# Last layer's four experts: twelve dense batch-expert tiles replaced by nine tiles of tokens grouped by expert through DRAM

## The reference, cut to what matters

```
xn = _modulate(_ln(x), sh_mlp, sc_mlp)
gate_logits = xf @ w_gate                                  # 4 experts
topk_logits, topk_idx = jax.lax.top_k(gate_logits, TOP_K)  # TOP_K = 2
gates = jax.nn.softmax(topk_logits, axis=-1)
cw = jnp.sum(jax.nn.one_hot(topk_idx, NUM_EXPERTS, dtype=xf.dtype) * gates[..., None], axis=1)
hmid = jax.nn.gelu(jnp.einsum('tc,ech->eth', xf, w1) + b1[:, None, :], approximate=True)
eo = jnp.einsum('eth,ehc->etc', hmid, w2) + b2[:, None, :]
moe = jnp.einsum('te,etc->tc', cw, eo).reshape(B, N, C)
return x + g_mlp[:, None, :] * moe
```

## Time and profile before

| | |
|---|---|
| median of 3 runs | 1899.22 us (1898.35 to 1902.36) |
| profiled execution, its own time | 1896.54 us |
| its span, first to last instruction | 1894.1 us |
| mean granted TensorE clock | 0.95 |
| last layer's feed-forward windows | 1372.5 us to the end |

### The profile page before, as it was taken

How to read it: one execution, slowest core, us unless ns; L and a number is a source line. 1 busy time by engine, 2 the same in 40 slices (tenths; PEclk the granted TensorE clock), 3 DMA queues, 4 the chain that set the end, 5 groups by cost and what they waited for, 6 DMA issues and landing times.

```text
span 1894.1 us, 27931 instructions
## 1 busy us (share of the span) xinstructions
PE 1738.4 (92%) x9838; PEld 1141.3 (60%) x9838; DVE 1159.2 (61%) x2573; ACT 914.4 (48%) x1635; POOL 577.1 (30%) x567
## 2 busy tenths in 40 slices
PE   6775899998998889998899999999999999999998
PEld 2443444433796634443378764444388899999997
DVE  7863677773555667677436567777445645455454
ACT  2323476667354468675745247676733322222221
POOL 4432122214555323332435232222523301101000
PEclk9997699999999889899899999998999899999999
DMA  7202333331001222323100223333110000100000
GB/s 245 79 2 71 95 105 91 91 112 48 11 1 51 91 82 72 90 70 114 57 11 1 88 67 109 92 100 114 39 38 19 20 25 20 44 10 29 1 26 25
DMA packets 65866, 116.49 MB, mean 61 GB/s; under 512 B 9443, under 2 KB 25235, under 8 KB 65439
## 3 DMA queue, kind: packets, MB, share of 16 engines
q1 hardware_dynamic: 65728, 114.71, 19.6%
HBM read 83.46 MB, written 30.73 MB: 60 GB/s over the span
## 4 chain that ended last, share of the span: by engine, by line
PE 70%; DVE 10%; ACT 7%; issue 4%; DMA 4%; POOL 4%; SPq 2%; DVEq 0%; ACTq 0%; POOLq 0%
PE ps L1696 25%; PE ps L1780 15%; PE ps L1749 8%; PE ps L1735 7%; PE ps L1844 6%; PE ps L1717 5%; ACT Pr L1545 2%; DMA heads_t<-stage 2%; PE ps L1820 1%; DVE negmax L1133 1%; ACT HQ L1520 1%; DVE GT L1059 1%; ACT act L1519 1%; ACT xn L1441 1%; PE ps L1586 1%
## 5 line engine op out<-in xcount | busy, mean ns | idle before, releaser
L1133 DVE TENSOR_REDUCE negmax<-ps 128x1 f32<-128x512 f32 x768 | 488.3, 681 | 221.3 <-PE ps L1717 218.0
L1545 ACT ACTIVATE Pr<-ps 128x512 f32<-128x512 f32 x768 | 410.6, 602 | 208.3 <-PE ps L1735 208.0
L1556 ACT ACTIVATE g<-ps,b1col 128x512 f32<-128x512 f32 x216 | 148.2, 688 | 449.1 <-PE ps L1696 445.0
L1322 DVE CAST G<-g 128x512 fp32r<-128x512 f32 x216 | 122.8, 568 | 280.7 <-ACT g L1556 280.2
L1735 PE MATMUL ps<-QK 55*128 55x512 f32 x768 | 239.5, 515 | 33.4 <-ACT Pr L1545 25.2
L1780 PE MATMUL ps<-W2a,G 128*128 128x288 f32 x1728 | 263.4, 302 | 4.8 <-DVE rowt L1143 4.8
L1780 PEld LDWEIGHTS ps<-W2a,G 128*128 128x128 f32 x1728 | 247.9, 192 | 19.1 <-DVE G L1324 7.3
L1749 PE MATMUL ps<-Pr,V 128*32 128x512 f32 x1536 | 220.0, 646 | 0.0
L1717 PE MATMUL ps<-QK 54*128 54x512 f32 x768 | 196.6, 444 | 18.7 <-DVE negmax L1133 7.0
L1735 PEld LDWEIGHTS ps<-QK 55*128 55x128 f32 x768 | 92.2, 192 | 198.7 <-ACT Pr L1545 103.5
L1324 DVE TENSOR_TENSOR G<-g,G 128x512 fp32r<-128x512 f32 x216 | 170.4, 789 | 7.4
(11 more groups left out here) (221 smaller groups left out, 2241.1 us busy)
## 6 DMA issues: line engine op xcount, KB each, us to landing
QK<-heads_t SPq DMA_DIRECT2D x192, 144.0 KB
heads_t<-stage SPq DMA_DIRECT2D x96, 252.0 KB
QK<-heads_t SPq DMA_DIRECT2D x192, 72.0 KB
raw<-in_w SPq DMA_DIRECT2D x18, 432.0 KB
raw<-in_w SPq DMA_DIRECT2D x12, 576.0 KB
WA<-in_ada_w SPq DMA_DIRECT2D x3, 1728.0 KB
heads_t<-stage SPq DMA_DIRECT2D x24, 144.0 KB
QK<-W1a SPq DMA_DIRECT2D x192, 2.0 KB
```

What stands on the lines that cost most here:

```text
L1133: dve.tensor_reduce(negmax[:, m % 2, h, t:t + 1], ps[:, row_bank(l, s, i), :], AX, ALU.max, negate=True).then_inc(a_free, 1)
L1322: dve.tensor_copy(G[:, n % 3, 0, :], g32[:, n % 2, :]).then_inc(g_hi, 1)
L1545: act.activation(Pr[:, t % 2, 2 * half + pair, :], ps[:, (16 * s + u) % 3, :], ACT.Exp, scale=SCALE).then_inc(b_free, 1)
L1556: act.activation(g32[:, n % 2, :], ps[:, hidden_bank(s), :], ACT.Gelu if l == 1 else ACT.Gelu_apprx_tanh, bias=b1col[:, e, s % FT:s % FT + ...
```

## The change

Batch 0 stays dense (all four experts), and batches 1 to 3 (1536 tokens, 3072 token-expert pairs) are grouped. The feed-forward part of the last layer has 13 windows in place of 16: windows 0, 1 and 2 are batch 0 with experts 0, 1 and 2; windows 3 to 11 are nine tiles of grouped tokens; window 12 is batch 0 with expert 3. Each of the 13 windows has weights of its own, so 13 sets of six pieces are loaded and split in place of 4.

Beside windows 0 to 2, for each batch 1 to 3: `modulate` writes the normed, modulated tokens in token order; the gate is computed turned round (7 matmuls of 512 columns, a copy, four small turns); `rank` counts, by two small matmuls, the place of each token in its experts' regions; `scatter` issues eight indirect DMAs from POOL that write each token's row into the region of each of its two experts in `tok_rows`, and waits for them. `table` then works out which expert and which rows each grouped tile has, and `slots` where each token's two results will be. Each grouped window loads 512 rows (`xg`), transposes them on PE (`lng`), runs as a tile with the weights that the table names, and stores its 512 result rows to `exp_rows`. In window 12, `gather` issues 24 indirect DMAs from POOL that fetch each token's two result rows, and `merge` adds them up on DVE, batch by batch. `tok_rows` (7680 rows of 1408 bytes) is filled with zeros in the prologue by one DMA.

```diff
+LAST, SEL = LAYERS - 1, B - 1
+GROUPED = 2 * SEL + EXPERTS[-1] - 1
...
+WINDOWS = (B, B, GROUPED + EXPERTS[-1])
...
+def raw_slot(n):
+    return n % 2 if n < THREE else (n - THREE) % 3
...
     if v == 0:
+        out += leaving(l) + [(4, "modrow", l, 1, 0), (12, "mod", l, 1, 0)]
+        out += [(14, "gate", l, 0, 0), (15, "gturn", l, 0, 0), (16, "gexp", l, 0, 0), (18, "weigh", l, 0, 0)]
+        out += [(16, "gate", l, 1, 0), (18, "gturn", l, 1, 0), (20, "gexp", l, 1, 0), (21, "rank", l, 1, 0), (23, "weigh", l, 1, 0)]
+        out += [(22, "scatter", l, 1, 0)]
+    if v == 1:
+        out += [(t // 2, "stats2", l, 2, t) for t in range(TT)] + [(2, "mean2", l, 2, 0), (0, "modrow", l, 2, 0)]
+        out += [(8 + c, "ln2", l, 2, c) for c in range(3)] + [(8, "mod", l, 2, 0)]
+        out += [(11, "gate", l, 2, 0), (13, "gturn", l, 2, 0), (15, "gexp", l, 2, 0), (16, "rank", l, 2, 0), (18, "weigh", l, 2, 0)]
+        out += [(17, "scatter", l, 2, 0)]
+        out += [(9 + t // 2, "stats2", l, 3, t) for t in range(TT)] + [(11, "mean2", l, 3, 0), (11, "modrow", l, 3, 0)]
+        out += [(15 + c, "ln2", l, 3, c) for c in range(3)] + [(17, "mod", l, 3, 0)]
+    if v == 2:
+        out += [(0, "gate", l, 3, 0), (2, "gturn", l, 3, 0), (4, "gexp", l, 3, 0), (5, "rank", l, 3, 0), (7, "weigh", l, 3, 0)]
+        out += [(6, "scatter", l, 3, 0), (6, "table", l, 0, 0), (10, "slots", l, 0, 0)]
+    if v + 1 < WINDOWS[l]:
+        first = PIECE["w1", l, v + 1, 0]
+        loads = {0: (-2, -2, 4, 6, 9, 11), 1: (0, 1, 2, 8, 10, 12), 2: (-3, -2, -1, 8, 10, 11)}.get(v, (-3, -2, -1, 8, 10, 12))
+        out += [(t, "load", l, first + q, 0) for q, t in enumerate(loads)]
+        out += [(t, "split", l, first + q, 0) for q, t in enumerate((5, 7, 9, 12, 14, 16) if v > 0 else (1, 3, 7, 9, 12, 15))]
+        out += [(9 if v > 0 else 16, "side", l, v + 1, 0)]
+    if i == -1:
+        out += [(12, "xg", l, 0, 0)] + [(15 + c, "lng", l, 0, c) for c in range(3)]
+    if 0 <= i < GROUPED - 1:
+        out += [(1, "xg", l, i + 1, 0)] + [(11 + 2 * c, "lng", l, i + 1, c) for c in range(3)]
+    if v == WINDOWS[l] - 1:
+        out += [(6, "gather", l, j, 0) for j in range(SEL)]
+        out += [(t, "merge", l, j, part) for j, t in ((0, 16), (1, 20), (2, 21)) for part in range(2)]
         out += [(21, "fin", l, v, 0)]
...
+            sp.dma_start(tok_rows.rearrange("(k p) c -> p k c", p=128),
+                         act32[:, 0, 0:CW].unsqueeze(1).broadcast_to([128, XROWS // 128, CW])).then_inc(zero_out, 16)
...
+            sp.wait_ge(zero_out, 16)
...
+            def tile_load(l, v):
+                sp.wait_ge(xs_out, ALL_XS)
+                if v >= 2:
+                    sp.wait_ge(misc_full, MISC["lng", l, v - 2, 2] + 1)
+                row = 0
+                if v > 0:
+                    sp.wait_ge(table_ready, 1)
+                    row = sp.value_load(tab[0:1, 1, v - 1:v], min_val=0, max_val=XROWS - N)
+                sp.dma_start(XG[v % 2][:, :, :], tok_rows[bass.ds(row, N), :].rearrange("(t p) c -> p t c", p=128)).then_inc(xg_in[v % 2], 16)
+            def tile_store(l, v):
+                sp.wait_ge(acc_free, TT * (WBASE[l] + FRONT + v + 1))
+                sp.dma_start(exp_rows[N * v:N * v + N, :].rearrange("(t p) c -> p t c", p=128), rowt[:, :, :]).then_inc(ys_out, 16)
...
+                elif kind == "scatter":
+                    pool.wait_ge(zero_out, 16)
+                    pool.wait_ge(mod_done, i)
+                    pool.wait_ge(idx_ready, i)
+                    for t in range(TT):
+                        for r in range(2):
+                            pool.indirect_dma_start(tok_rows, bass.IndirectOffsetOnAxis(idx[:, i - 1, t, r:r + 1], 0),
+                                                    XG[(i - 1) % 2][:, t, :], None).then_inc(xs_out, 16)
+                    pool.wait_ge(xs_out, 16 * 2 * TT * i)
+                elif kind == "gather":
+                    if i == 0:
+                        pool.wait_ge(ys_out, 16 * GROUPED)
+                        pool.wait_ge(slots_ready, 1)
+                        pool.wait_ge(misc_full, MISC["lng", l, GROUPED - 1, 2] + 1)
+                        pool.wait_ge(acc_full, TT * (WBASE[l] + FRONT + GROUPED))
+                    for t in range(TT):
+                        for r in range(2):
+                            pool.indirect_dma_start(GA[i][r][:, t, :], None, exp_rows,
+                                                    bass.IndirectOffsetOnAxis(yidx[:, i, t, r:r + 1], 0)).then_inc(yg_in[i], 16)
+                    if i == SEL - 1:
+                        for j in range(SEL):
+                            pool.wait_ge(yg_in[j], 16 * 2 * TT)
...
+            def merge(j, part):
+                first, second = GA[j]
+                if part == 0:
+                    dve.wait_ge(yg_in[j], 16 * 2 * TT)
+                    for t in range(TT):
+                        dve.tensor_scalar(first[:, t, :], first[:, t, :], cws[:, j, t, 0:1], None, ALU.mult).then_inc(dve_done, 1)
+                        step()
+                    dve.wait_ge(dve_done, steps[0])
+                    for t in range(TT):
+                        dve.scalar_tensor_tensor(out=first[:, t, :], in0=second[:, t, :], scalar=cws[:, j, t, 1:2],
+                                                 in1=first[:, t, :], op0=ALU.mult, op1=ALU.add).then_inc(dve_done, 1)
+                        step()
+                    return
+                xb = X[:, TT * (j + 1):TT * (j + 2), :]
+                dve.wait_ge(dve_done, steps[0])
+                dve.wait_ge(mlp_in, mlp_in_total(LAST))
+                dve.tensor_tensor(first, first, bc3(gbc[:, j + 1, :], TT), ALU.mult).then_inc(dve_done, 1)
+                dve.wait_ge(dve_done, step())
+                dve.tensor_tensor(xb, xb, first, ALU.add).then_inc(merged, 1)
+                dve.wait_ge(merged, j + 1)
...
+            def rank(l, b):
+                n, j = MISC["rank", l, b, 0], b - 1
+                dve.wait_ge(misc_full, n + 1)
+                if j == SEL - 1:
+                    dve.tensor_copy(tot[:, :], ps[:, 7, 4 * TT:4 * TT + 4]).then_inc(dve_done, 1)
+                    step()
+                dve.tensor_tensor(place_in[:, j], ps[:, 7, 0:4 * TT].rearrange("p (t e) -> p t e", e=4),
+                                  bc3(ebase[:, :], TT), ALU.add).then_inc(misc_free, 1)
+                dve.tensor_scalar(pen[:, j], chosen[:, :, :], FAR, FAR, ALU.mult, ALU.subtract).then_inc(dve_done, 1)
+                dve.wait_ge(dve_done, step())
+                dve.wait_ge(misc_free, n + 1)
+                for r, (op, best) in enumerate(((ALU.subtract, ALU.min), (ALU.add, ALU.max))):
+                    dve.tensor_tensor(seen[:, r], place_in[:, j], pen[:, j], op).then_inc(dve_done, 1)
+                    step()
+                dve.wait_ge(dve_done, steps[0])
+                for r, best in enumerate((ALU.min, ALU.max)):
+                    dve.tensor_reduce(lohi[:, :, r:r + 1], seen[:, r], AX, best).then_inc(dve_done, 1)
+                    step()
+                dve.wait_ge(dve_done, steps[0])
+                dve.tensor_copy(idx[:, j], lohi[:, :, :]).then_inc(idx_ready, 1)
+                dve.wait_ge(idx_ready, j + 1)
...
+            def modulate(l, b):
+                mb = XG[(b - 1) % 2]
+                dve.wait_ge(xn_ready, NORM["mean2", l, b, 0] + 1)
+                dve.wait_ge(modr_in, 32 * b)
+                dve.wait_ge(misc_full, hq_over(l, B - 1))
+                if b == 3:
+                    dve.wait_ge(xs_out, 16 * 2 * TT)
+                dve.tensor_tensor(mb[:, :, :], xn[:, :, :], bc3(modr[:, 1, :], TT), ALU.mult).then_inc(dve_done, 1)
+                dve.wait_ge(dve_done, step())
+                dve.tensor_tensor(mb[:, :, :], mb[:, :, :], bc3(modr[:, 0, :], TT), ALU.add).then_inc(mod_done, 1)
...
+            def table():
+                dve.wait_ge(setup_done, 16)
+                dve.tensor_scalar(filled[:, :], tot[:, :], 0.0, None, ALU.is_gt).then_inc(dve_done, 1)
+                dve.wait_ge(dve_done, step())
...
+                dve.tensor_copy(tab[:, :, :], where[:, :, :]).then_inc(table_ready, 1)
...
+            def slots():
+                places, far = (x[:, :, :, :].rearrange("p b t e -> p (b t) e") for x in (place_in, pen))
+                weights_ = cw[:, 1:B].rearrange("p b t e -> p (b t) e")
+                dve.wait_ge(fin_done, WBASE[LAST])
...
+                if kind == "lng":
+                    pe.wait_ge(xg_in[i % 2], 16 * (i // 2 + 1))
+                    rows = 128 if k < 2 else 96
+                    for t in range(TT):
+                        ins = pe.transpose(bank[0:rows, 128 * t:128 * t + 128], XG[i % 2][:, t, 128 * k:128 * k + rows], ident[:, :])
+                elif kind == "rank":
+                    pe.wait_ge(chosen_set, i)
+                    pe.wait_ge(setup_done, 16)
+                    ones = onecol[:, 0:1].broadcast_to([128, 128])
```

(11 more changed lines are left out.)

438 lines of the change are left out of this document (338 added, 100 removed).

## The result

The changed kernel is slower, by 0.7%. Its median is 1913.77 us (1908.04 to 1924.94, 20 runs) against 1899.79 us of the kernel before on the same chips (1891.97 to 1917.02, 20 runs): ratio 1.0071, 95% interval 1.0053 to 1.0088. Forecast were 1859 us and a gain.

A forecast was written before the change was run, and what follows sets the result against it. PE's matmul work was taken as the bound. Start of window 1, windows 1 and 2, grouped windows and tail: 1415.9 + 111 + 270.3 + 57 = 1854.2 us of span, a median of 1859 us; 8-in-10 range 1828 to 1888.

The forecast's parts named there:

- Gate and window 0: Turned-round gates take 2 us each with no clock fall; window 0 stays at 43.3 us.
- Windows 1 and 2: From window 1's start to window 3's: 65 us plain, 42 for scatters, 4 for the lower clock, 111 us together.
- the clock's 4: In windows 1 and 2, 4 us added for the lower clock after PE's long waits.
- An indirect DMA: On POOL, 1.05 us each, plus 2.5 us for landing after the last; one scatter of eight blocks POOL 10.9 us.
- Grouped windows: Nine windows bound by PE at 29.1 us, plus transposes in eight: 270.3 us; weights and transfers cost nothing.
- Rival 3: Grouped windows not PE's: POOL's blocks hold DVE's `G` up, 3 us lost in each of nine, 1886 us; 12%.
- Window 12 and the tail: From window 12's start to the end: 24 gathers, three merges, `finish` and output stores, 57 us against 39.4.
- 1, POOL quick: An indirect DMA costs POOL near 0.28 us, each scatter 6 us shorter, 1840 us; 20%.
- 2, indirect DMAs held up by DVE: Each indirect DMA on POOL waits out DVE instructions, costing 2.4 us: 1926 us; decides at a cost of 1.88 us; 10%.
- 4, the fill: Filling `tok_rows` in the prologue is not hidden; at half the rate it costs 12 us, 1871 us; 6%.

The follow-up runs named there:

- e9: e5 with all three W2 remainders ahead of scatter 2, POOL's power earlier, `weigh` and `slots` later, first grouped transposes retimed; windows 1 and 2 107.2 us, ratio 0.9930.
- e1: Changed kernel with scatter 1 moved behind batch 2's norm and scatter 2 a little later in POOL's list; median 1892.35 us, windows 1 and 2 117.5 us.
- e5: Changed kernel with windows 1 and 2 reordered at once (scatters, W2 remainders, rank ahead of `finish`, first grouped load first); windows 1 and 2 114.8 us, ratio 0.9981.
- e6: e1 with SP's first grouped load ahead of three weight loads; windows 1 and 2 114.1 us, ratio 0.9992.
- e12: e10 with `weigh` and `slots` moved behind `finish` and POOL's power behind the first grouped rows; 143.7 us to window 4, ratio 0.9848.
- after again: The changed kernel, unchanged, profiled a second time; windows 1 and 2 130.5 us, tail 63.9 us, execution 1897.47 us.
- e10: e9 with the last window's `finish` ahead of batch 3's merge and the first grouped transposes one tick later; tail 56.7 us, ratio 0.989.

## Why the prediction was wrong, step by step

From window 0's start, the prediction's own terms make 481.7 us against the 521.6 of before; measured were 532.9, 51.2 us more than the sum. Four terms were too small: window 0 by 4.7 us, windows 1 and 2 by 20.3, the grouped windows by 11.6, window 12 and the tail by 14.7.

**Gate and window 0 (2 us a gate, "no clock fall from it"; window 0 left at 43.3 us, measured 48.0).** The gate's own price was nearly right. Both gates of window 0 ran at the full clock, and those of batches 2 and 3 at the lower level, right behind PE's waits of 12.48 and 15.67 us (their rows are above):

```profile
1419.99 1.78 PE L2122 MATMUL ps<-HQ,Wg 128*4 128x512 f32 x7
...
1426.03 1.79 PE L2122 MATMUL ps<-HMv,Wg 128*4 128x512 f32 x7
```

and by stretches (PE, PEld, DVE, ACT, POOL busy, granted clock, DMA share, GB/s):

```profile
1420.00:1429.20 9.20, 9.20 (x54) 6.77 (x54) 8.92 (x26) 3.37 (x5) 8.87 (x4) 1.00 0.32 95
1468.36:1471.50 3.14, 3.14 (x8) 1.23 (x9) 0.00 (x0) 0.00 (x0) 1.70 (x4) 0.50 0.40 128
```

So the new gate took 1.79 us and its turns 1.05, 2.8 us for the 2 of the sum, and 4.2 us behind a long wait; the low clock came with the wait, not with the gate's shape (in e9 the gate of batch 3, behind a wait of 2.27 us, took 1.79). Window 0's 4.7 us are something else: 2.8 us of waiting for ACT's GELU and for DVE, of which window 0 had none before, 0.6 us more work, and 1.3 us of low clock at its start in this execution (with the first hidden group at 1.9 us in place of 3.23, as in e1 or e9, it takes 46.7 us). The sum had put those waits at nothing; what brings them was not tested.

**Windows 1 and 2 (111 us; measured 131.3).** This is the term that failed most. Where PE waits was right, place by place: PE's gate of batch 2 waits for POOL's remainders (11.6 us said, 12.48 measured), batch 3's again (12.4 and 15.67), SP's load waits for what follows scatter 3. The sizes were off. In us after window 1's start:

```
                      said    measured
scatter 1 begins      12.0      12.4
gate(2) begins        34.9      39.1
window 2 begins       49.0      60.2
scatter 2 begins      49.2      64.8
gate(3) begins        61.4      77.8
scatter 3 begins      79.0      98.3
scatter 3 landed      90.0     110.1
window 3 begins      107.0     131.3   (111 with the clock's 4)
```

The three scatters account for 4.8 of the 20.3 us (14.1 + 11.6 + 11.8 for 3 x 10.9). The step that failed is the one ahead of scatter 2, on which the gate of batch 3 hangs. The sum had POOL at work without a break from the first remainders to scatter 2, 14.3 us; the trace has 25.8, and 10.4 us of them are three waits for ACT's copies:

```profile
1475.53 2.03 POOL L1083 TENSOR_TENSOR W2a<-raw,W2a 128x864 fp32r<-128x864 f32 x1 [5.22 <-ACT W2a L1756]
1479.92 2.01 POOL L1083 TENSOR_TENSOR W2a<-raw,W2a 128x864 fp32r<-128x864 f32 x1 [2.36 <-ACT W2a L1756]
...
1489.14 1.29 POOL L1134 TENSOR_TENSOR HMv<-act,HMv 128x512 fp32r<-128x512 f32 x1 [2.84 <-ACT HMv L1944]
```

In ACT's list the copies of `W2a` stand behind GELUs of hidden groups that PE ran only after the gate of batch 2, and that gate had waited for POOL. So a wait went round from POOL to PE, to ACT and back to POOL, and the slow gate and the hidden group behind it (3.14 and 2.54 us) lengthened it. The rows that scatter 2 writes were not ready before 62.7 either. PE's own lateness at window 2 (60.2 for 49.0; 2.57 us of it a wait for `xn`, which ACT made behind one of these GELUs) cost nothing directly: PE waited 15.67 us at the next gate. Beyond that, it was 2.9 us more than said from the gate of batch 3 to scatter 3 and 4.2 us more from its landing to window 3; against this stand the 4 us put down for the clock.

I had added the clock as one lump of 4 us and left these chains out. e1, e5, e6, e9 and e12 show that the order of the lists was worth 23 us to window 4, as much as the error of this term: I saw the queue and priced it, and didn't ask whether the sum would still carry the change with a small slip in each term.

**An indirect DMA (1.05 us, landing 2.5).** Mis-sized: 1.09 + 0.30 in the scatters, 1.00 + 0.30 in the gather; 1.63 us from the last one's end to POOL's going on. That 1.05, taken from another instruction of POOL, came so near to the issue itself is luck. The 0.30 us between two of them was in no row of before and in neither term. The Trainium skill, page "DMA: Bandwidth & Descriptors", section "Anatomy of one DMA", gives about 2.0 us fixed for a transfer; here it was 1.63 us from the end of the last issue and 2.6 from its start (scatters 2 and 3), on either side of that figure.

**Grouped windows (30.1 us; the first as the others).** 31.0 us: transposes and a 0.32 us wait for POOL's last remainder are 1.9 us and not 1.05. The first took 35.7, with 2.97 us of waiting for `G` behind this row of DVE, beside two of POOL's W1a remainders (1572.40 to 1578.36):

```profile
1572.06 6.62 DVE L1401 SCALAR_TENSOR_TENSOR X<-rowt,cw,X 128x288 f32<-128x288 f32 x4
```

Together 281.9 for 270.3, +11.6. Rival 3 named a loss of 3 us in every window by POOL and DVE holding one another up; it struck one.

**Window 12 and the tail (57 us; measured 71.7).** 56.4 with plain loads: the parts other than the gathers were right as a sum. 24 gathers took 31 to 34 us and not 25.2, which is 7 to 8 us with what follows (63.9 in after again). The other 7.8 us of the profiled execution go with the standstill, which no part of the prediction had.

**Rivals.** 1, POOL quick: refuted. 2, indirect DMAs held up by DVE: there, but small. The longest took 1.96 us where 0.96 is the rule (first row fence of POOL above), the mean of 1.39 us stays under the 1.88 us at which it was to decide, and the kernel is slower all the same: that bound held only if all else in the sum was right. The Trainium skill, page "SBUF — State Buffer", section "SBUF: two separate sides", names the lock, with ~3100 ns for a DMA so held up; 1.97 us (after again) is the most that a run here shows. The hold-up that cost more is the opposite one, DVE's steps beside POOL's long ones (e10's rows). 4, the fill: hidden, as forecast.

**The range** ended at 1888. Its bounds were the price of one operation; the error was made of four slips of the same sign (4.7 + 20.3 + 11.6 + 14.7), most of it waits that were left out.

**Not settled:** the standstill, and how much slower the changed kernel is. From window 0 on its profiles are 11.3 us longer than before's with the standstill and 1.8 without; timed it is 14 us. After again's one execution took 1897.47 us, under the lowest of the 20 timed (1908.04) and under before's median on its chip (1905.83). Either most executions have the long standstill, or a part of the difference lies ahead of window 0, where its scatter of 20 us hides it.

## What to carry to other kernels

When work is saved by sending rows through DRAM, price the indirect DMAs on the engine that issues them and then read, in that engine's list, what stands behind each block, and for each entry when its inputs come (10.4 us of POOL's list here were waits for ACT): here the same operations ran 0.7% slower or 1.5% faster than before by the order alone. Expect each wait that is removed to give back a part at the next queue; after each reordering read the waits up to one window beyond. In a tail, put what needs no gathered rows (`finish`) into the wait for the last of them: 7 us from e9 to e10.

## What the runs showed of the hardware

A 128-row indirect DMA of 1408 or 1152 bytes a row cost POOL 0.95 to 0.96 us undisturbed and 0.30 us to the next, in either direction, and 1.97 us at most. A 128x16 multiply on DVE took 2.03 us beside POOL's 128x864 subtraction, and 0.17 us alone. ACT stood still for up to 16.9 us (e5) and PE for up to 2.4 us between single matmuls, in 5 of the 10 executions profiled with a row of 24 gathers that nothing held back; the cause is unknown.
